# Linear attention's values loaded in one DMA over 128 partitions, and the order of turns drawn anew

## The chip, the cores and the metric

The kernel runs on one core of one Trainium2 chip. The metric is device time in microseconds; before the change the median of three runs is 1362.3 us (1359.67 to 1363.4). The core's engines are TensorE (PE), VectorE (DVE), ScalarE (ACT), GpSimd (POOL) and SyncE (SP, which here issues nearly all DMAs). Each takes its own instructions in order and waits on semaphores for the others.

## The reference

Eight batches of 256 tokens with 128 channels go through two layers; each layer adds two branches to its input. All is float32.

```
xn = layernorm(x)
x  = x + gla(xn) + local(xn)          # layer 0
xn = layernorm(x)
x  = x + delta(xn) + experts(xn)      # layer 1

gla (gated linear attention), per head (H = 4, Dk = 16, Dv = 32):
  S  = exp(gt)[..., None] * S + kt[..., None] * vt[..., None, :]
  ot = einsum('bhk,bhkv->bhv', qt, S)
  o  = rmsnorm(o) * g_norm_w * silu(x @ Wg);  return o @ Wo
local: two layers of windowed attention with a gated MLP
delta: delta rule in chunks of 32, two gates, state S passed from chunk to chunk
experts (8 heads, 8 experts, top 2 of 8 for values and for outputs):
  v   = einsum('bshep,bshe->bhsp', einsum('bsd,hedp->bshep', x, v_w), gate_v)
  att = softmax(q k / sqrt(P));  ctx = att v
  out = einsum('bshep,hepd->bsd', ctx[:, :, :, None, :] * gate_o[..., None], o_w)
```

## The kernel before, in words

**Gated linear attention.** The recurrence runs over time in the free dimension: for each pair of value channels j, j+1 one tile kv (128 partitions x 2 x 256) holds the values, repeated for each of the 16 key channels. Its 128 partitions are (half of the value channels, head, key channel): 2 x 4 x 16. ScalarE writes the values v of a batch to a tile, SP sends them to DRAM (`values`, L1775) and loads them back, repeated, into one of four kv tiles (`kvload`, L1791). VectorE multiplies by k (`gkv`, L1115) and scans over time with the decay (`gmul`, L1123, two scans), GpSimd multiplies by q (L1698), and TensorE sums over the key channels with a constant matrix `gla_sum` (L760, one group for two tiles). A batch has eight kv tiles; the loads of the fifth to eighth wait until the L760 group that reads the slot's earlier tile has run.

**Experts.** For each head and half of the experts (16 units for a batch, 128 in all) SP loads router weights repeated over all partitions, `vgate<-gates` (L1821) and `ogate<-gates` (L1833), and expert weights `wv`, `wo`. Three slots exist for each. GpSimd multiplies vgate by the input (L1748), TensorE makes the values (`hv`, L899, letter V), runs the attention (L910, L917, L927, L936, letter A), VectorE multiplies the context by ogate (L1352), and TensorE makes the output (`mproj`, L946, letter P). A V frees the value slot, a P the output slot, and only then SP issues the next load of that slot.

**Delta rule.** For each of the eight chunks TensorE's `du` (L827, state x winvT), VectorE's two products (L1294, L1296), TensorE's `ds` (L827, dlt x vkC), VectorE's sum into the state (L1305) and the next `du` follow each other; `dout` adds the output.

**The order.** No dependency sets the order of an engine's instructions: five strings do (TENSOR_TURNS, VECTOR_TURNS, SCALAR_TURNS, GPSIMD_TURNS, SYNC_TURNS). Each letter takes the next stage of one stream: a, b, c the local branch, G the linear attention, C the router, F and D the delta rule, A, V, P (W, O, v, o on the other engines) the experts, z the end of layer 0, E the store. BANK_TURNS gives each TensorE stage its PSUM bank. An engine that comes to a stage whose input is not there waits, with all that is queued behind it.

Of the kernel before, what the change touches and what calls it, by code (L numbers as in the profile page):

```python
# [37 lines left out]
def constants():  # L38

    i, j = np.arange(P)[:, None], np.arange(P)[None, :]  # L40
    out = {"ident": (i == j), "headsum": (i // DK == j // DK)}
# [46 lines left out]
    "VDaaDADDaaDaDDVDADDaAPPDbbDDaVDADDbaDaDDVDGaDDAVbbVDAbAbaPDAbbPFAbGbAAaAbVPPcaGVAcabAAVAPPcGbEaAbcAAGVGGacAaVG"
    "VAbbabbFFaPbAAbFAbPbVAbacGDaVcPaAAcVAPaVcAacPzPAAVAaCGaCVAPbAAaPbGPAPCVVVbbAabAAabAabVbFAGbaPbAAbGAbPDDcDaVDGc"
    "aDAVDDPDDAADcADDaVbbADPDDGbDVDDcDPDDAADaADDaaVDGAVFFDcGazPbbEbbFGPbbAAVbbAbDVPAVcCGVcGPVAAcPACVcAPPAAcAaPaCaAa"  # L90
    "AAPAPFPAaAAaAGPPADDaabVbVDaAADbVADDGGDVDAVVDDaDPDDAAaVbPbDDbDADbVDDbDDbaDbDDbabGDaAFaaPVAAaabbDAaPGGEbGFaPAFAA"
    "aVbbbAbPDbVbPbbcbGAcVPAAcVAcVAPccAAPcGAVcacAVcPzaAAPACGVCaPAVaaAAPVCGAaVbabPPDDAFADAabAVaDVGaDDGPDbbPDDbDbDDbb"
# [6 lines left out]
    "aaGbGbbcacbbcGbbaabccccaazGCCcaacGbcabbCCCbACCCCACGacccaGGcGzGCbCaGbbGGbGVCCCCCCCCVAOAVVOFcaaVVFcaacOFAOVVGGAF"
    "aaGbGabOaOGVVbAGbGGAFFFFDDbOOAbFVVADbcccbcGOOaaAVVAaaGFOAFAOFcOOVVcFcAVVAFFFFaaAFDAcccbDaDbbaVVDODbGDDDDODGDcb"  # L100
    "DGGbbDGDGDbGDGDaaGGDaOODADAcaVVGGcGcGaaDDGAaAaGVVGGDEbObbOcccabOOcAAzCCabOObACbCACbCCCCVVCaOOAaAFaaFDaVVGaGFDa"
    "DbcaDFbbOOVVbDDGDAcAcDDFDDFDOODGDGAGGAGDGGcccDGDGbVVDOObDcDzbVVCDbDCAFAFFEDOOcAaAaVVccVVOOAACCCCOOVVCCaCAaCAaa"
    "VVGGGGcccOcOAGDAGGGDDDaDaDDaaVVDODODbDbbDADbDAaDaVVDaDabDbDVVODbOAbAFFOOAaFAacFVVcbcabOOGAaAbEGbOOcVVccGcAAVVG"
    "bGGbbGGabaOFOAaAFGaGFGGFcFDGVVcGcDaOaOAGGADVVccccaazaCOOCAACCVVCCCOCCOCbAGGbbAGVVGbabOObAabAaVVbFFaOODAaFDAGcD"
    "FDcDcaVVDGaDODAOADbDbbDGDbVVDccDcDODOADaAaDDDVVFFczCCbEFbbFGbOGFGAGGAGGVVGGODDcaacDcGGVVOGGAOCCACCCcccCCVVOcAC"
    "AOGaaGOaAOAGaGFOOAaADaFFbDaaFVVbbDODObADADGVVDVVDDOObDDbDADbAVVDbDDaDaDaGDaFaDabOAabbAGEObaFFFOVVbOAbbFADDbDcc"
    "GVVcGGGOGAOAGGGVVcccGccOOccAAGaacccGVVGcGzCaCOaAOACCCCCVVCCCGGaAaOVVbOADbbGGbaDaFFDFVVDODAOFbDAGDbDbDDbDDDOODF"
    "DDGFDVVDGDFDAFADDFcDVVOOAcAcEVVOcccAOAczCCFVVOFACOACFCCCVVOCAOACFCVVDOOFDAFDAFFDFDVDVODODADADDDDVDVODODADADDDD"
# [12 lines left out]

GPSIMD_TURNS = (
    "aaaaaaababGGbabaGaGaGaaGaaGGbbbbGaaaaaaabaGbGGGabaabaGGaaGaaGbbbabaaGaaababaGWGWWbbGGWWWWaWWaaaGWaWabaGWabWGGb"
    "DWDDDDDWbDWWWaWaaDaDWaWaGWDbaDDbDaWDDDDDDbGDDGDDbGDaaGaWaWaDaGaGWWDbaGDbGDDbDWbDWaDaDaaWaWaDGaDbaWbWDDDDDDDDDD"
    "WGDGGDDGWbWbWDWDDDDWWWDWDDWDaWaaGDaDWDDaDaaDaGDWGDWDbDGDbDWDaDaaWDaWbWbaWaWabWaGbWWbWGabaGaaGGWDGWaWaDWaGaDDWW"
    "DDbGWbGDbDbDaWaaWaDWDDWDGaDWDDaDbWDbDDWDDDDaaWWbbGWGGGWDWDDDDDGDaDaGaGDaGaWWaWbaDaDWWWbDDWDWWDDDWbDDDDbDWDDaaa"
    "GaaaWbabaWbbDWDDWGGWGGWDDaWaDWaGaDWGDGaDWWWbbaaGDaDWDWDDbDDDbDDDWDDDGDWWDWWDWDWWDWWWDDDDDDWWDDWDDDDDWDDDDWDDDW"
    "DWDWDWDDWDWDDDWWWDDDDDDWDWDDDDDDDD")

SYNC_TURNS = (  # L130
    "xxxGGGGGGGGGGGGGGGGGGGGGGGCvvvooovvvGGvCvvGGoovvoovvovvoovvooovovvvvovoGGGGGoGGovvGGvvooEoxoooovoovCoovvvvooGG"
    "GGGvoovvvovoExoovvvoovvooGGvvGGCoovvoovvvvoovoovvooExvGGGvGGvoovGGvovovoovGGvooooCvvvvoovvovovovvGGGGoGEoxvvov"
    "GGvGGovovoooCooooovvvvvvovovovoEoGGvGGGovovovvooGGvvooGGvooCvvvoovvoovovvvvvovvEovvvoooooooCvvvoovoovvoovvovoE"
    "oovoovvoovvoooovvoooE")
# [10 lines left out]
    "26531746273514275425712347135131753175147157354514351403754130754107354107451347310473140143147137437140371437"
    "01475032471504750514765427507415743150714530745307451374105374105734073407354057034703543474357405764035764576"
    "37567304307634706343706370363760367103465710457031245013650136401340130173415347163471564731654016530615360143"
    "605463705167420536172506132706531705361750321573152071352703725")
# [1778 lines left out]
```

## Time and profile before

| | |
|---|---|
| median of 3 runs | 1362.3 us |
| the profiled execution | 1362.17 us |
| its span, first to last instruction | 1360.8 us |
| mean granted TensorE clock | 0.951 |
| PE, DVE, POOL, ACT busy | 89%, 71%, 62%, 53% |
| DMA engines: share of q1, bytes in all | 52.3%, 230.88 MB |

Shares are of the span. DMA share in a stretch is the mean over the core's 16 DMA engines. The granted clock is a share of 2.4 GHz: at 1.0 TensorE runs at 2.4 GHz, at 0.5 at 1.2 GHz. The chain of waits is followed back from the last instruction, at each step to what released it.

### The profile page before, as it was taken

Reading aid. Unit: us, or ns where it says so; the run is one execution under the profiler, and the core shown is the slowest. Engines: PE = TensorE matmul, PEld = TensorE weight load, DVE = VectorE, ACT = ScalarE, POOL = GpSimd, SP = SyncE. Lnnn points to the kernel's source line nnn. Section 1 sums busy time; section 2 is a strip of 40 time slices with the busy share of each in tenths; the row PEclk is TensorE's granted clock in tenths of the full one; section 3 lists DMA queues with packets and bytes.
Section 4 is the critical chain, followed back from the end, with each engine's and each line's share of the span. In section 5 each row is a group of like instructions: output and inputs, shape, how many; then the busy total and the mean of one; then the engine's idle time right before and its main releaser. Section 6 shows DMA issues by size and latency. Waiting matters only on the chain.

```text
span 1360.8 us, 31248 instructions
## 1 busy us (share of the span) xinstructions
PE 1207.0 (89%) x11890; PEld 955.2 (70%) x11890; DVE 962.8 (71%) x1950; ACT 722.1 (53%) x2060; POOL 847.7 (62%) x1157
## 2 busy tenths in 40 slices
...
GB/s 241 34 26 42 12 237 196 165 193 142 126 154 221 129 175 145 280 154 183 175 152 190 240 108 172 188 190 190 164 125 194 168 217 135 219 217 248 250 279 112
DMA packets 90675, 230.88 MB, mean 170 GB/s; under 512 B 9376, under 2 KB 15648, under 8 KB 90400
## 3 DMA queue, kind: packets, MB, share of 16 engines
q1 hardware_dynamic: 90384, 228.30, 52.3%
...
## 4 chain that ended last, share of the span: by engine, by line
PE 38%; DVE 25%; DMA 13%; ACT 12%; issue 7%; POOL 4%; SPq 1%; DVEq 0%; ACTq 0%; POOLq 0%
PE bank L899 9%; PE bank L946 8%; DMA ogate<-gates 7%; DVE ogate L1352 5%; DMA vgate<-gates 3%; PE bank L827 3%; DMA kv<-values 3%; DVE dy L1210 3%; PE bank L612 2%; ACT prob L1463 2%; PE bank L917 2%; PE bank L936 2%; POOL vgate L1748 1%; PE bank L927 1%; PE bank L707 1%
## 5 line engine op out<-in xcount | busy, mean ns | idle before, releaser
L1748 POOL TENSOR_TENSOR vgate<-vgate,xT 128x512 f32<-128x512 f32 x256 | 329.3, 1311 | 144.5 <-DMA vgate<-gates 144.2
L899 PE MATMUL bank<-wv,vgate 128*128 128x128 f32 x2048 | 264.4, 285 | 3.5 <-POOL vgate L1748 3.2
L899 PEld LDWEIGHTS bank<-wv,vgate 128*128 128x128 f32 x2048 | 254.6, 200 | 11.4 <-issue 6.8
L946 PE MATMUL bank<-ogate,wo 128*128 128x256 f32 x1024 | 251.6, 393 | 3.4 <-DVE ogate L1352 2.0
L946 PEld LDWEIGHTS bank<-ogate,wo 128*128 128x128 f32 x1024 | 195.2, 196 | 40.7 <-issue 14.3
L1352 DVE TENSOR_TENSOR ogate<-ogate,bank 128x1024 f32<-128x1024 f32 x128 | 153.3, 1213 | 49.6 <-DMA ogate<-gates 30.5
L1463 ACT ACTIVATE prob<-prob,mx 128x128 f32<-128x128 f32 (+1 forms) x256 | 96.0, 377 | 72.9 <-DVE mx L1059 72.7
L1630 ACT ACTIVATE mprob<-bank,mmin 128x256 f32<-128x256 f32 x128 | 59.4, 468 | 133.2 <-DVE mmin L1341 133.0
L1681 POOL TENSOR_TENSOR rot<-rot 128x512 f32<-128x512 f32 x64 | 81.7, 1277 | 65.5 <-DVE rot L1035 65.5
L612 PE MATMUL bank<-wqkv,hT 128*128 128x512 f32 x192 | 108.1, 664 | 4.5 <-ACT hT L1399 2.8
L1726 POOL TENSOR_TENSOR dlt<-dlt,step 128x126 f32<-128x126 f32 (+22 forms) x248 | 95.5, 385 | 19.4
L1698 POOL TENSOR_TENSOR kv<-kv,gq 128x512 f32<-128x512 f32 x64 | 82.3, 1291 | 33.8 <-DVE kv L1123 33.8
L1724 POOL TENSOR_TENSOR step<-dlt,uw 128x126 f32<-128x126 f32 (+22 forms) x248 | 90.9, 366 | 19.4 <-DVE dlt L1275 3.1
L1693 POOL TENSOR_TENSOR prob<-prob,rsum 128x256 f32<-128x256 f32 (+1 forms) x64 | 60.7, 951 | 57.7 <-DVE rsum L1062 57.5
L1688 POOL TENSOR_TENSOR rot<-rot,rn 128x512 f32<-128x512 f32 x64 | 68.8, 1075 | 28.1 <-ACT rn L1447 27.8
L1123 DVE TENSOR_TENSOR_SCAN kv<-bank,kv 128x256 f32<-128x256 f32 x128 | 81.0, 674 | 1.2
L936 PE MATMUL bank<-mprobT,vmoe 128*128 128x256 f32 x256 | 69.6, 395 | 6.0 <-ACT mprobT L1645 4.3
L917 PE MATMUL bank<-xT,mqk 128*128 128x256 f32 x256 | 69.0, 392 | 4.9 <-DVEq L1359 2.5
L1637 ACT ACTIVATE mprob<-mprob,msum 128x256 f32<-128x256 f32 x128 | 57.8, 500 | 26.3 <-DVE msum L1346 26.0
L1620 ACT ACTIVATE mqk<-bank 128x256 f32<-128x256 f32 x64 | 24.4, 381 | 74.5 <-PE bank L910 74.3
L1645 ACT ACTIVATE mprobT<-bank 128x512 f32<-128x512 f32 x64 | 37.9, 593 | 46.0 <-PE bank L927 45.5
L627 PE MATMUL bank<-small,rot 128*128 128x128 f32 x256 | 41.9, 288 | 20.4 <-POOL rot L1688 9.8
...
## 6 DMA issues: line engine op xcount, KB each, us to landing
vgate<-gates SPq DMA_DIRECT2D x128, 512.0 KB, 4.3
ogate<-gates SPq DMA_DIRECT2D x128, 512.0 KB, 4.4
wv<-in_wv_moe SPq DMA_DIRECT2D x128, 256.0 KB, 4.7
wo<-in_wo_moe SPq DMA_DIRECT2D x128, 256.0 KB, 4.9
kv<-values SPq DMA_DIRECT2D x128, 128.0 KB
...
x<-in_x SPq DMA_DIRECT2D x8, 128.0 KB, 3.2
```

Of the source, the lines that this page charges most:

```text
L612: nc.tensor.matmul(out, m.hT[:, n * P:(n + 1) * P], m.wqkv[:, l, k * INNER:(k + 1) * INNER], start=True, stop=True).then_inc(bank.filled, 1)
L899: i = nc.tensor.matmul(out[:, n * D:(n + 1) * D], xg[:, e, n * P:(n + 1) * P], m.wv[slot][:, e, :], start=(q, n, e) == (0, 0, 0), stop=(q, ...
L917: i = nc.tensor.matmul(out[:, n * T:(n + 1) * T], m.mqk[:, n * P:(n + 1) * P], m.xT[b % 2][:, :], start=True, stop=True)
L936: i = nc.tensor.matmul(out[:, 0:T], m.vmoe[:, k, h % 2, :], m.mprobT[:, k, :], start=k == 0, stop=k == 1)
L946: i = nc.tensor.matmul(out[:, 0:T], m.wo[slot][:, e, :], cg[:, e, :], start=(h, q, e) == (0, 0, 0), stop=(h, q, e) == (MH - 1, 1, EQ - 1))
L1352: i = tt(gate, gate, spread(out, 1, EQ), ALU.mult)
L1463: e = act(p[:, c, :], p[:, c, :], ACT.Exp, scale=-1.0, bias=top[:, c:c + 1], accum_out=rsum[:, c:c + 1])
L1681: tt(r, r, r2, ALU.add).then_inc(s.rot_added, 1)
L1698: tt(kv, kv, spread(m.gq[:, :], 1, 2), ALU.mult).then_inc(s.gmul, 1)
L1724: g.chain(tt(step, spread(m.solved[:, k // 2:, k], 2, k), spread(m.lanes[:, k, 0:k], 1, rows), ALU.mult))
L1726: i = tt(left, left, step, ALU.subtract)
L1748: i = tt(gate[:, e:e + half, :], gate[:, e:e + half, :], spread(m.xT[b % 2][:, :], 1, half), ALU.mult)
```

## The change

It has two parts. The first changes how the values come into the kv tiles. The partitions of kv are now (key channel, half, head), so that the repetition over key channels is the outermost dimension and one DMA fills all 128 partitions; the columns of the weights for q, k, the decay and v, and the matrix `gla_sum`, are put in the same order on the host. The second draws all five order strings and the bank string anew; each letter comes as often as before on every engine.

```diff
-    half, head = np.arange(P) // (GH * GK), np.arange(P) // GK % GH
+    half, head = np.arange(P) // GH % GVH, np.arange(P) % GH
...
 TENSOR_TURNS = (
-    "GaaaaGGGaaaaabbaXabbbbbaaaabbGbaabGbaaabbacaGGGbbcbbbbcbcbbcGbaaacGGGaacGaaabbccaabcGbbbaaabGbbaaaaabbGbabbcaG"
+    "GaaaaGGGaaaaabbXababbbbaGbababbabacaaacabGGbcacabGGcbbbaaabGbbaabbaaabbbGGaGcbGabcbbbcbcbGcbbGabaacaacGaaacbbc"
...
-        v.wait_ge(s.kv_in[slot], 32 * use)
+        v.wait_ge(s.kv_in[slot], 16 * use)
...
-        for a in range(GVH):
-            src = values_dram[b % 2].rearrange("(h a j) t -> a h j t", h=GH, a=GVH)[a, :, j:j + 2, :]
-            dst = m.kv[slot][a * GH * GK:(a + 1) * GH * GK, :, :]
-            nc.sync.dma_start(dst, spread(src, 1, GK)).then_inc(s.kv_in[slot], 16)
+        src = values_dram[b % 2].rearrange("(g j) t -> g j t", j=GJ)[:, j:j + 2, :]
+        nc.sync.dma_start(m.kv[slot][:, :, :], spread(src, 0, GK)).then_inc(s.kv_in[slot], 16)
...
-    twice = lambda w: np.tile(w, (1, GVH))
+    twice = lambda w: np.tile(w.reshape(-1, GH, GK).transpose(0, 2, 1)[:, :, None, :], (1, 1, GVH, 1)).reshape(-1, P)
...
-    a["gkb"] = np.tile(f["L0_attn_gk_b2"], GVH)[:, None]
-    a["gk1"], a["wv_gla"] = f["L0_attn_gk_w1"], f["L0_attn_Wv"]
+    a["gkb"] = twice(f["L0_attn_gk_b2"][None, :]).T
+    a["gk1"], a["wv_gla"] = f["L0_attn_gk_w1"], f["L0_attn_Wv"].reshape(D, GH, GVH, GJ).transpose(0, 2, 1, 3).reshape(D, P)
```

Two places of the order. The first is SP's queue where the first four kv tiles of the sixth batch are loaded (`x2` are the two halves of a tile; vgate and ogate with wv and wo are the loads of the experts). Before:

```order
L1821 DMA vgate0<-gates 128x1024
L1822 DMA wv0<-in_wv_moe 128x512
L1791 DMA kv0<-values 64x1x512 x2
L1791 DMA kv1<-values 64x1x512 x2
L1821 DMA vgate1<-gates 128x1024
L1822 DMA wv1<-in_wv_moe 128x512
L1791 DMA kv2<-values 64x1x512 x2
L1791 DMA kv3<-values 64x1x512 x2
L1833 DMA ogate0<-gates 128x1024
L1834 DMA wo0<-in_wo_moe 128x512
```

The same tiles in the changed kernel:

```order
L1819 DMA vgate1<-gates 128x1024
L1820 DMA wv1<-in_wv_moe 128x512
L1789 DMA kv0<-values 128x1x512
L1789 DMA kv1<-values 128x1x512
L1789 DMA kv2<-values 128x1x512
L1789 DMA kv3<-values 128x1x512
L1831 DMA ogate0<-gates 128x1024
L1832 DMA wo0<-in_wo_moe 128x512
L1831 DMA ogate1<-gates 128x1024
L1832 DMA wo1<-in_wo_moe 128x512
```

The four tiles now come together in four DMAs of 128 partitions, the vgate load that stood between them comes ahead, and two ogate loads follow.

The second is TensorE's queue where the first batch leaves layer 0 (`small,xn` is a transpose of normalized inputs, `gla,go` the linear attention's output, `xT,w_qk` and `xT,mqk` queries and scores of an expert head, `layer,xT` the router, L798). Before, up to the router:

```order
L779 MATMUL bank<-gla,go 128x128 x2
L910 MATMUL bank<-xT,w_qk 128x256
L647 MATMUL bank<-qkT 64x64 x8
L647 MATMUL bank<-qkT 64x128 x8
L752 MATMUL bank<-xn0T,gla 128x256
L917 MATMUL bank<-xT,mqk 128x256 x2
L732 MATMUL bank<-xn0T,gla 128x256
L733 MATMUL bank<-xn0T,gla 128x256
L798 MATMUL bank<-layer,xT 128x128 x2
```

In the changed kernel:

```order
L591 MATMUL bank<-small,xn 128x128 x2
L772 MATMUL bank<-gz,gla 128x256
L612 MATMUL bank<-wqkv,hT 128x512 x3
L591 MATMUL bank<-small,xn 128x128 x2
L779 MATMUL bank<-gla,go 128x128 x2
L752 MATMUL bank<-xn0T,gla 128x256
L910 MATMUL bank<-xT,w_qk 128x256
L671 MATMUL bank<-probT,vloc 64x64 x8
L798 MATMUL bank<-layer,xT 128x128 x2
```

The router matmul moves from row 136 to row 122 of TensorE's order: local attention of the second batch (L647, L627, L612, L691) that stood ahead of it now comes later.

## Rows read from the trace of the kernel before

**Rows 1.** busy time of the engines over the span, from the page
```profile
PE 1207.0 (89%) x11890; PEld 955.2 (70%) x11890; DVE 962.8 (71%) x1950; ACT 722.1 (53%) x2060; POOL 847.7 (62%) x1157
```

**Rows 2.** busy us of each engine by stretch, granted clock, DMA share, GB/s
```profile
0.00:200.00 200.00, 147.41 (x1152) 98.81 (x1153) 142.69 (x323) 146.11 (x440) 99.75 (x95) 0.88 0.27 97
200.00:1300.00 1100.00, 1004.46 (x10032) 811.14 (x10032) 792.95 (x1571) 560.46 (x1579) 722.30 (x1015) 0.96 0.58 182
```

**Rows 3.** the chain by line, shares of the span, from the page
```profile
PE bank L899 9%; PE bank L946 8%; DMA ogate<-gates 7%; DVE ogate L1352 5%; DMA vgate<-gates 3%; PE bank L827 3%; DMA kv<-values 3%; DVE dy L1210 3%; PE bank L612 2%; ACT prob L1463 2%; PE bank L917 2%; PE bank L936 2%; POOL vgate L1748 1%; PE bank L927 1%; PE bank L707 1%
```

**Rows 4.** long pieces of the chain that ended last: start, us, what
```profile
51.32 6.39 DMA kv<-values
...
222.84 10.63 DMA ogate<-gates
...
574.55 9.05 DMA kv<-values
...
887.11 15.13 DMA ogate<-gates
...
1090.46 9.39 DMA vgate<-gates
```

**Rows 5.** the same chain near 887 us, in full
```profile
881.25 0.53 SPq L1791
...
886.22 0.84 SPq L1791
...
902.27 1.23 DVE ogate L1352
```

**Rows 6.** PE in order of time, 897 to 907 us
```profile
897.72 1.89 PE L707 MATMUL bank<-hn,local 128*128 128x256 f32 x8
903.70 2.00 PE L707 MATMUL bank<-hn,local 128*85 128x256 f32 x4 [4.09 <-DVEq L1359]
```

**Rows 7.** DMA issues: KB each, median us from issue to landing
```profile
vgate<-gates SPq DMA_DIRECT2D x128, 512.0 KB, 4.3
...
kv<-values SPq DMA_DIRECT2D x128, 128.0 KB
```

**Rows 8.** landings of the ogate loads (L1833), min, median, max
```profile
DMA to landing us min/median/max: 3.5/4.4/15.1
```

**Rows 9.** two stretches of one us: kv loads alone, gate loads at full rate
```profile
29.00:30.00 1.00, 0.00 (x0) 0.00 (x0) 0.80 (x5) 1.00 (x4) 0.98 (x1) 1.00 0.27 98
...
221.00:222.00 1.00, 1.00 (x6) 0.89 (x5) 0.95 (x2) 0.00 (x0) 0.74 (x1) 1.00 1.09 432
```

**Rows 10.** eleven stretches around long waits for loads
```profile
222.00:239.00 17.00, 13.75 (x71) 10.22 (x70) 14.45 (x25) 9.56 (x22) 9.53 (x8) 0.91 0.73 238
...
887.00:908.00 21.00, 14.19 (x64) 11.14 (x64) 14.80 (x23) 6.16 (x15) 17.00 (x41) 0.77 0.73 213
...
sum 173.00, PE 137.08 PEld 109.67 DVE 124.34 ACT 81.39 POOL 95.56; mean PE 12.46 PEld 9.97 DVE 11.30 ACT 7.40 POOL 8.69
```

**Rows 11.** who waited for loads, us in total, times, longest
```profile
DVE kv L1115 <- DMA kv<-values: 22.9, 11, 4.9
```

**Rows 12.** PE's own waits: us in total, times, longest
```profile
PE bank L827 <- DVE dlt L1296: 7.5, 10, 2.8
...
PE bank L827 <- DVE state_sum L1287: 5.5, 4, 2.6
...
PE bank L827 <- POOL dlt_sum L1734: 4.9, 2, 4.5
PE bank L760 <- POOL kv L1698: 4.7, 3, 2.2
```

**Rows 13.** a stretch of the start, busy us
```profile
160.00:180.00 20.00, 13.71 (x88) 10.48 (x87) 17.13 (x48) 19.46 (x58) 6.69 (x7) 0.87 0.19 66
```

**Rows 14.** issue times of kv loads on SP (ns)
```profile
L1791 SPq DMA_DIRECT2D kv<-values x128: 509/511/1887, 21.1 to 1089.9; - x128
```

**Rows 15.** the output matmuls, busy and mean, idle before them
```profile
L946 PE MATMUL bank<-ogate,wo 128*128 128x256 f32 x1024 | 251.6, 393 | 3.4 <-DVE ogate L1352 2.0 <-DVEq L1358 1.3
```

More of the change, by code:

```diff
@@ L88 @@
[L88 to L92, printed above, removed]
@@ new lines @@
+    "DADGaDaaAbbaDDbacDGVbbVcaDDPAEAbcAPPbbVAbPbbVPAAGcAPPAVcaVzGaAAaAaGPVPAaaGVCVFAAaaAaCVaVPAPAAVAaVFFPADDbGGbDbG"
+    "bbbcDPbcDDAbVcbbDPcDDbbDcDDbzDADDbbDCGDDbADFDDPDAcDDAAVDAVcVPDDAVAAcVAPPEPCAVAACVAPPGcAVaAAaAaaPcPAVaaAACVAGaa"
+    "bPbaPAaVbAAaVbbbbaPbaPAabVbbaaabAcbbVcAGAFcAPcPDcDbVADGGDVDDADAVDDADPDDaDADPDDVDDaDGDDADAaVDDADaPbbbbAGVGGGbbD"
+    "AAFbbAFbPVEaFGVcGaADaVGcVaaPcPAAaVbbAGGaVbGPaVAaPAAcAGcVzAPaAbbbCPbCAabPbPbAbabFcCaacGAGAAVcAVcVPaPcADDAAzVDAa"
+    "DaPDbbDAPDaAbDDAaDADDFDaDFDDPDDADFDDAADGAVDDPaADVbbbbVDDbPbAbbAVbAcGCGPPEAcPAAVAcVCVcPVAcAAVAPPPACVAAVAPPAaVAA"
@@ L95 @@
+    "aAaaPAPAAGFAaaPPaAabbaVDDbaVGDAADGaDPbbbbAPbbDDGDDabbADabDDaDVDDaDaDDaDGbVbDADDAabDDPAaacDaFAVbbbbDcPDVbbEAbbA"
+    "cFbAcVAGFcGVcaVcaaPcGAVAVAcPPVcAaazAAVAPVaACabbCaPFAAPAaVVbAaPbbbbAAPbACVbVbPbAVbAAPAFFDDFVDGAVDVDDGcDVDDPDcVD"
+    "DPDADDAGDADDcVDPDDADGGDDAAVDAGPcDDAGVcPzVAACVACPPEPAVAAFACVPPAVAAVAPPFAFFAAAPPVDDAVDADADVDDADDPDPDDADVDDADADDV"
+    "DADDPDPDDAVDAAVPDDAPVVAAAAPPAEAAAPPAAAVAPPAAAAPPDADVDVAADVADDPDPADDVAADVADDPDPADDVAADVADDPDPADDVAADVADDPDPAADP"
     "PE")
 VECTOR_TURNS = (
-    "VaaaaaaaGaabaabbabGGabGGGbbaabGGaaGGGaaGGGaabGGGbbcbbcGbbcbccccGaacGaacaacbGaabbGGGbGcccGGcGbGaabGbaabGGGaaGGa"
@@ L99 @@
[L99 to L108, printed above, removed]
@@ L122 @@
-GPSIMD_TURNS = (
[L123 to L128, printed above, removed]
+    "VaaaaaaaGaabaabbaGGGbGbaGGbbGGbaaGGaaGGcacabcaabbGGGGbccccbGbaabGaabaabaabbGcGcGbbcGbGbGGbGGGccccGGaaGGcaaGcGG"
@@ new lines @@
+    "acaGbaaabbcccczaCGCGaabbGaaCCCaabCCCabaaCbACFFaAbFcbbGcFcaVVabGGaaGcccOOcGGzGCAGCAbGVVFbFaabaabOOAFGAFGbGFVVbb"
+    "GGbGcGOCcCCcCCObCVVCAbCAbDDGbDVVOOAAOOVVAAcccFcOFcVVFcaaAFcaaAOGVVcccaaOcAOAbaabbGODbOFFDAGDADDDGDFDbDaDaGDGDa"
+    "aGGDbbVVDGGODAOAbFaDaGFGDaaGGcDGDbDcVbbDDcbVGEGGADAObGGabOabVVbOOcccAAcVzVCCaaOAaaOAGaaVVGFFAaaOAOFVVCCCFVVCAO"
+    "ACOFDFCCDGCDbcbbDcbDOcbODVVbccDcbDcDbzDDDDGDACDAGCGDGGDcFGGDADOVDVcAGcFDDVVOOOGFAEAVVDOOACCaACaCCCcccCOOVVaaAC"
+    "AaacGGGGaaOOVVAbaaAGbbGGGbOOVVbbbaabaaAAaacbVcbbcVOObAFDcccAFFcDDFDGVDVODODADADDaDaDVDVDDGODODADADbDGbbVVbOGOF"
@@ new lines @@
+    "AGGGGGGGGaaVVAFGGGGcaaGDGcDcGGaaFEOOVbVFbbAabaaFAGGDOVOVcccAGcAzCCObVOVabbCCCbCCCCCAacAaFcacOOAaVVFAFcccDcFDOz"
+    "ODVAVCDaAaCbDbbDObDODaDADaDFAFDDDFDFDAOOADGFGDGDbDVbbVGDDbGGGGGOVVOAcDAGGGcGcGGGGAOAVVCCCCCcccCCVcVCOOAOAEVVOO"
+    "AaAaVVOOAaAaaaOOFAaAaFbDabbaFbDVVDODODFbGAbbADbDGaDaDDaaDDDaDabGVVDbbDOObDaaAAcDDDbcFbbDDcbVVEOOFAAcccFFcFVVcD"
+    "cacaOaVaVOGAGGAGGcccGGVVGGczaaOOACACVVbaabbCCCbCCACOACOCVbVFbbOAbOFAVFVFOODAFFADFFDVVFDGDGGGDcDGGDcGGDcDVDVODO"
+    "DAADDDDVVOODADGGDADDcccGDczCCOVOVACCCAECCCCCVVOAOAFFFVVOOAFAFFFVVOOAFDAFDDVDVODODADADDDDVDVODODADADDDDVVODODDA"
@@ new lines @@
+    "DAVVOOAAEVVOOAAOOAAOOADADVVDODOVVADADDODOVVADADDODOVVADADDODOVADADDDOOE")
+SCALAR_TURNS = (
+    "GaaaaaGGGaaaaGaaabaaababaXbbbabbabaabbbaaacaacaabcaaabcabGaGbabbGaabbbaaaababaabbGGaaaGacGbcbbbbcbbcbabbabaaca"
+    "aaacaaacbaacaaaGGaCGabCbaaCAaaaabaababGGGbaaAFbbCaaabbbAbacAFcaGFbcaacaAabFCAAbAabaaFbaabAbabbAAbFbbAbCcCaacba"
+    "AbcbbAAbbACbAbbAAbAAAAcAFAaacFcaaAGcaaAGFcAaaAaaAaAbaAaaGbAFDFDbAGAGGAaaGabaabbaabaAbbAaAaAFbaabbaaacDDbacbEAb"
+    "cAAbAbbabbAcAAAaCaAaaGAaaAGAaaGCFAaaaCAaAaaAFAFaAAFAFDDbGbbGbbcbbccbbbcbbbAbbCGbGACAAcADADcAAFAcEAACAACAaAcAaA"
+    "aaAaAAaaaaACaaaAbaAabAabAaabbbabbaabaAabbAabaAaacbcAbcFAcADDbFAGGFAAAaAaaGAaAaDADabbbAGbGGbbAFGbbAbEaaAFaAcaac"
+    "aacAaabGaFGbbAaAaGAaAcAAACaaCbbbCbbbAabbabFACcAaAaGGcAcAaacAaFADFDAaACaAabAbbaAFAaAaaFAAGAFAGaADDbbbbbbbbAbAcC"
+    "AEAcAcACAcAAAAACAAaAAaAaAAaAaAaaFaaAAaAaabDbDbaaaFAaaGGFbbbAbbbAGbabAbaaaaaaaabbbAaaAaAaaDAcDFbbbEcbbbbbAcbFAA"
+    "cAGGFacacacaGAaaGAcAAaaAACAaACaabCabAaFaAAbAabbbAbbCAbAbbAFbAFFADDAFAFccAcAAAGGADGDAAcACACCEAAAAFCAAAAFAFAFAFA"
+    "AFADDAAAAAAAAADDAAAAAAAEAAAAAAAAAAAADADAAAAAAAAAAAAAAADDAE")
@@ new lines @@
+GPSIMD_TURNS = (
+    "aaaaaaabaGbGGbGbaaGaaGaaabaGGbbaaGabaaaababGbGbGGGaaGaaGaaGabaGabaaaabaaabWWWbabaGaWaWWGGGbWaaabaGWGWbbGWbWDGb"
+    "DWWDDWWDWWDaDaaWaaWaDaDaGbbDDDDDDDaDaDGaDaGDbWWGDDbaDaGDaaGWbWDGGbDDWDWDGDWaWaaDaaWWaWaDaWWDbbGDbDbDDbDDDbDDDD"
+    "DDWDDWWGWGWGWWGWDDWWDDaWaaDaaWaWabaGbDDabaabaWDaGaWDWGGbbWDDWDDWDDWDDaDDaDDDGWDDWbbWGGGGaWaGGaWaGWaGWabWabaDGW"
+    "DDDDbWbDDaWaaDaWDWWDDWaDabDbDDaDDDaDDDDDDWGWbbWGGGDWDDDWGWWDWGWDGGWWDaDaaWaDaaabWabDWDDbDbDGaDDaDaDaDDWaDabDDW"
+    "baDaWbbWWDWDWaDWWaaDWaaWaDWababDWWbDbDWDGWGWGDGDWDWDWDGDWDGDGDWDDGDDDWDGWDDDWDWDWWDDDWDWWWDDDWDDWDDDDDDWDDDWDW"
+    "DWDDDDDDDDWWWDWDWDDWDDWDDWDDWDDDDD")
@@ L130 @@
 SYNC_TURNS = (
[L131 to L134, printed above, removed]
+    "xxxGGGGGGGGGGGGGGGGGGGGGGGCvvvooovvvoovGGGGovvoovvovCvoovvvvooovvooooGGGGGvvGGGGvvoEoxovovooovvovovvvvoooGGGGG"
@@ L137 @@
+    "ooCvvvovvvovvooEovxvooGGvoovCvGGoovvoovvoovvvoovvovGGGGGovGGvGGvvooEvxvovovooooCGvGGGGvvoovooovovvovGGGGooovvv"
+    "ovvoEooCxvvoovoooovvoovvovovEvGvGGGGvovvoovvovoovvooCvvovovGGvvGGvovovovovovvooEovCvoovvoooovvvoovvoovvoovvooE"
+    "oovoooovvvoovvoovoooE")
 BANK_TURNS = (
-    "76543210765204375643275062743503764257602356702367531072613051236750123675021435026742035425603742560372536053"
-    "76250735067502316705316072015637201560253064571320473215760140673740653174065317460517345174573670631756070156"
@@ L145 @@
[L145 to L148, printed above, removed]
+    "76543210765204375643275037265403726507365270632532072536017253617205365204136750124507351243601243560124356012"
```

33 lines of the change are left out of this document (12 added, 21 removed).

## The prediction

> **What bounds the kernel now.** I read the page's engine line first, then the stretches, then the chain of waits, then the pieces of that chain that are loads.
>
> TensorE is the bound: busy 1207.0 us of 1360.8 [rows 1], so 153.8 us idle. The stretches [rows 2] put 200 − 147.4 = 52.6 us of that in the first 200 us and 1100 − 1004.5 = 95.5 us between 200 and 1300. Its granted clock is 0.88 in the first stretch and 0.96 in the second, that is, part of the time at 1.2 instead of 2.4 GHz; (1 − 0.96) × 1100 = 44 us of the second at full-clock worth are lost too. No work is taken from TensorE by this change, so a gain can come only from these two: idle time and clock.
>
> The chain by line [rows 3] names the matmuls of the experts (9% and 8%) and, right behind, loads: ogate<-gates 7%, vgate<-gates 3%, kv<-values 3%. The pieces in order of time say which loads. Eleven pieces of the chain are waits of over 7 us for a load that was issued right behind a group of kv loads, or for kv loads themselves; first, longest and last are in [rows 4], the eleven sum to 107.9 us, the longest is 15.13 us. The reader is to see in [rows 5] what stands before the longest: eight kv issues of L1791 from 881.25 to 887.06, with one gate load between, then an ogate load that lands 15.13 us after its issue, and in [rows 6] TensorE idle for 4.09 us until VectorE's product with that ogate. The median for the same kind of load is 4.3 us [rows 7], its extremes 3.5 and 15.1 us [rows 8].
>
> Why: while kv loads run alone the DMA share is 0.27 at 98 GB/s, and while gate loads run it reaches 1.09 at 432 GB/s [rows 9]. 0.27 is close to four of sixteen engines (0.25), though two halves of a kv load, issued 0.5 us apart, are in flight together. So both halves take the same four engines, and a gate load that needs all sixteen ends behind them.
>
> By the Trainium skill, "DMA: Bandwidth & Descriptors", section "Why a DMA increments its semaphore by 16 and not by 1", a DMA takes the largest number of engines, at most 16, that divides both sides' slowest dimension, and always the lowest-numbered ones. The source of a kv load has 4 heads outermost, so 4 engines, the same for both halves: the trace agrees with its 0.27. The new source has the 16-fold repetition outermost and the destination 128 partitions, so 16.
>
> **What the change does, part by part.**
>
> 1. kv loads: 128 DMAs of 128 KB on four engines become 64 of 256 KB. The same bytes. Four old DMAs (two tiles, 512 KB, the usual group) take 512 KB / 98 GB/s = 5.3 us of four engines; spread as the gate loads are, whose destination also has 128 partitions outermost, they go at up to the 432 GB/s of [rows 9] and take 1.2 us of sixteen. A gate load behind such a group is up to 4.1 us earlier. SP issues 64 DMAs fewer at 0.51 us [rows 14], 33 us in all; SP mostly waits for free slots, so I cost this at nothing, except that each gate load behind a pair of tiles leaves 1 us earlier, which the 4.1 us contain roughly.
>
> 2. What that is worth on TensorE. In eleven stretches around those waits (wait, and a few us behind it; first, longest and sum in [rows 10]) TensorE is busy 137.1 of 173 us, 79.2%; in the rest of 200 to 1300 it is (1004.5 − 137.1) / (1100 − 173) = 93.6%. So the long waits cost 173 × 0.936 − 137.1 = 24.8 us of idle time, and about 5 us of clock (the clock of the eleven is short by 12.6 us in sum, where the average of the rest would give 5.9; both times 0.8 busy). 30 us against 107.9 − 11 × 4.35 = 60 us of landing over the median: half a microsecond of TensorE per microsecond of lateness. Nine of the eleven are gate loads: 9 × 4.1 × 0.5 = 18 us at best. Several lie where gate loads also queue behind each other (DMA share 0.73 in both stretches shown), which the change leaves, so I take two thirds, −12 us, and keep 0 and −25.
>
> 3. Waits for kv itself. VectorE waited 22.9 us in eleven times for kv loads [rows 11]; two are in the eleven pieces above (one is the 9.05 us of [rows 4]), and 51.32 in the start is a third. From 9.05 and 6.39 us to the 4.3 us of a gate load of twice the size. VectorE is not the bound; TensorE shows only 4.7 us of waiting for the products of kv [rows 12]. Bounds 0 and −12; I take −5, near the TensorE row.
>
> 4. The start. Before, the order gives TensorE about 119 us of matmuls (group means times counts) ahead of the first router matmul L798, now 108; the second batch's moves from 143 to 187. So expert work starts earlier, by at most 11 us of work, in a stretch where TensorE is 74% busy, which would bring 11 × 0.26 = 3 us. But ScalarE is busy 19.5 of 20 us there [rows 13], so it could also come to nothing, or cost a little if the chain rather than TensorE sets the start. −3, bounds +4 and −8.
>
> 5. Spacing of the experts. Three slots serve the gate loads, so an output product P (L946) can come only when the load issued behind the third P before has landed and been multiplied. Counted in matmul time from the order, 8 of 125 P had under 10 us for this, now 4; for the value matmuls 3, now 1. TensorE waited only 3.4 us before L946 [rows 15]: −2, bounds 0 and −4.
>
> 6. The delta chain. Between a chunk's L827 du and its ds, TensorE needs VectorE's two products; 20 of 56 pairs had under 2 us of other matmuls between, now 26. One such wait is 7.5 / 10 = 0.75 us [rows 12]. Six more: +4.5 us at most, +2 taken, 0 to +8 kept.
>
> Constants, weights and bias columns only change their contents: nothing. The wait count 16 for 32 is the same wait.
>
> Sum: −12 − 5 − 3 − 2 + 2 = −20 us. The profiled execution took 1362.17 us, 1.4 us around its span of 1360.8, and the median of the runs is 1362.3. 1362.2 − 20 = **1342 us**.
>
> **Rivals.**
>
> A. The loads were hidden, gain under 0.3%. For it: all loads of a kind wait behind slots, and SP spent its time waiting for products, not issuing; if a gate load lands 4 us earlier and TensorE still idles for VectorE or ScalarE (which between them make most of the entries in its wait list), only the bare TensorE waits go: 4.7 us for kv, and the drawn order returns +2 or more. About 1360 us. Against: the 4.09 us of [rows 6] sit directly behind a load. This is also what would come if the new loads did not use sixteen engines: then the plan, which counts on early kv tiles (in the sixth batch the third L760 group follows the first by 10 us of matmuls, before by 46), would wait, and it might be 1365.
>
> B. Slower: the delta chain is the new wait. Its place is L827, seven rounds for each batch, du, VectorE, ds, VectorE, du. The three largest waits at L827 are 7.5 + 5.5 + 4.9 = 17.9 us [rows 12]. If they grow by more than the count of tight pairs, say by half, and the POOL part too, that is +9 us, and ds behind a late du holds every expert matmul queued behind it on the in-order TensorE. It decides once the loads give less than 9 us: with a gain of 3 us from loads and nothing at the start, 1362 + 9 − 3 = 1368 us. Against: before, six of the eight tightest pairs lay in the last 300 us, where TensorE was as busy as elsewhere.
>
> C. More than forecast. If item 2 comes at its full 25 us, item 3 at 12 and the start at 8, less the +2: 1362 − 43 = 1319; half of the extra gives 1325. For it: after the long waits the chain holds more waits of 4 to 6 us for gates, which shrink a bit too, and less idle time keeps the clock at 2.4 GHz.
>
> **How the numbers follow.** Forecast (1328 to 1356): 0.58. A: 0.16. B: 0.14. C (below 1328): 0.12. The range 1326 to 1367 leaves out half of C and most of B, under 2 in 10. A measurement of this kernel tells 0.3% (4 us) from no change: below 1358.2 is faster, above 1366.4 slower. Faster 0.58 + 0.12 + 0.02 of A = 0.72; same 0.13; slower 0.14 of B and a little of A, 0.15.
>
> **What would show it.** Item 1: a stretch in which kv loads run alone shows a DMA share near 1, not 0.27, for a quarter of the time; the longest landing of ogate falls from 15.1 to some 10 us. Item 2: the chain holds less of ogate<-gates than 7% and fewer than eleven load waits over 7 us; TensorE's idle time between 200 and 1300 us falls from 95.5 to about 80. Item 3: VectorE's wait for kv falls from 22.9 to under 10 us. Items 5 and 6: waits before L946 no longer, before L827 up by a few us. I am wrong if landings fall and TensorE's idle time does not, or if it moves to L827 or to the first 200 us.

## The result, and the profile after

| | before | changed |
|---|---|---|
| median of 4 runs | 1361.0 us (1357.3 to 1363.4) | 1291.3 us (1287.8 to 1297.5) |
| ratio, 95% interval | | 0.9495 (0.9449 to 0.9541) |
| profiled execution, span | 1362.2, 1360.8 us | 1297.5, 1295.0 us |
| mean granted TensorE clock | 0.951 | 0.979 |
| TensorE idle | 153.8 us | 119.4 us |

The change takes 70 us, 5%, off; the forecast was 1342 us with a range down to 1326. The direction was right and the size was far off.

The busy line of the changed kernel, which answers to [rows 1]:

```profile
PE 1175.6 (91%) x11890; PEld 930.8 (72%) x11890; DVE 971.2 (75%) x1950; ACT 721.9 (56%) x2060; POOL 851.1 (66%) x1157
```

The span shrinks by 65.8 us, in two nearly equal parts: TensorE's idle time falls by 34.4 us, and the same 11890 matmuls take 31.4 us less busy time. The fall in busy time is the clock: busy time at a granted clock below 1, weighted by what is missing to 1 and summed over windows of 2 us, is 57.7 us before and 25.1 us now, 32.6 us less. The stretches, as in [rows 2] (busy us of the five engines, granted clock, DMA share, GB/s), show where it rose:

```profile
0.00:200.00 200.00, 152.74 (x1173) 101.78 (x1174) 153.08 (x336) 151.64 (x445) 108.17 (x100) 0.91 0.32 110
200.00:1235.00 1035.00, 967.50 (x10058) 783.34 (x10056) 789.94 (x1560) 556.14 (x1578) 724.53 (x1030) 0.99 0.59 191
```

The clock of the long stretch goes from 0.96 to 0.99, its idle time from 95.5 to 67.5 us. The window of one us in which only kv loads run, against the first row of [rows 9]:

```profile
26.00:27.00 1.00, 1.00 (x12) 0.98 (x10) 1.00 (x3) 0.96 (x6) 0.23 (x1) 1.00 1.02 287
```

The DMA share is 1.02 where it was 0.27, so all sixteen engines carry the load. The issues and the landings of the ogate loads, as in [rows 7] and [rows 8]:

```profile
vgate<-gates SPq DMA_DIRECT2D x128, 512.0 KB, 4.5
...
kv<-values SPq DMA_DIRECT2D x64, 256.0 KB, 4.5
```
```profile
DMA to landing us min/median/max: 3.6/4.2/10.2
```

The median landing of the gate loads hardly moves (4.4 to 4.2 us for ogate); the longest goes from 15.1 to 10.2 us. The waits of VectorE for loads, as in [rows 11] (us in total, times, longest):

```profile
DVE kv L1115 <- DMA kv<-values: 9.0, 5, 3.5
...
DVE ogate L1352 <- DMA ogate<-gates: 2.1, 3, 1.4
```

Before, the second of these was more than the 22.9 us for kv:

```profile
DVE ogate L1352 <- DMA ogate<-gates: 30.5, 13, 5.6
```

TensorE's own waits, as in [rows 12] and [rows 15]:

```profile
PE bank L946 <- DVE ogate L1352: 6.7, 6, 3.1
PE bank L827 <- DVE dlt L1296: 4.8, 9, 1.1
PE bank L827 <- DVE winvT L1279: 4.8, 3, 2.4
PE bank L760 <- POOL kv L1698: 3.2, 2, 3.0
```

L946 waits more than before (the group of [rows 15] had 3.4 us of idle time ahead of it, now 7.7), L827 less. The chain of this execution could be followed back for the last 890 us only (its shares add up to 68%); a second profiled execution of the same kernel, of 1288.2 us, has a whole one. Its shares by engine, and those by line, against [rows 3]:

```profile
PE 49%; DVE 34%; ACT 9%; issue 5%; DMA 2%; POOL 1%; DVEq 0%; ACTq 0%; POOLq 0%
PE bank L899 11%; PE bank L946 10%; DVE ogate L1352 5%; PE bank L827 4%; PE bank L612 4%; PE bank L936 3%; DVE kv L1123 3%; DVE dy L1210 3%; PE bank L917 2%; PE bank L927 2%; PE bank L671 2%; PE bank L647 2%; DVE kv L1115 1%; DVE prob L1055 1%; PE bank L707 1%
```

DMA is 2% of the chain where it was 13%, and no load is left in the list by line. Of the eleven pieces of over 7 us ([rows 4] has the longest) one has a successor; the longest loads of this chain are:

```profile
0.73 4.45 DMA gla<-in_gla
...
661.25 4.66 DMA kv<-values
...
1053.84 8.39 DMA kv<-values
```

### The profile page after: what moved, and what is told of

Read it like the earlier page. It is cut to its first block, busy times and chain, and to the rows that moved or that the text cites. A ratio compares the mean times of both kernels' runs of the same rounds, so it can differ in the third digit from the quotient of the medians.

```text
span 1295.0 us, 31167 instructions
## 1 busy us (share of the span) xinstructions
PE 1175.6 (91%) x11890; PEld 930.8 (72%) x11890; DVE 971.2 (75%) x1950; ACT 721.9 (56%) x2060; POOL 851.1 (66%) x1157
## 4 chain that ended last, share of the span: by engine, by line
PE 32%; DVE 24%; ACT 5%; DMA 4%; issue 3%; POOL 0%; DVEq 0%; ACTq 0%; POOLq 0%
PE bank L899 8%; PE bank L946 6%; DVE ogate L1352 5%; PE bank L827 3%; PE bank L936 2%; DVE dy L1210 2%; DVE kv L1123 2%; DMA kv<-values 2%; PE bank L612 2%; PE bank L917 1%; PE bank L927 1%; DVE mmin L1341 1%; PE bank L647 1%; DMA ogate<-gates 1%; PE bank L671 1%
## 5 line engine op out<-in xcount | busy, mean ns | idle before, releaser
L899 PE MATMUL bank<-wv,vgate 128*128 128x128 f32 x2048 | 257.5, 280 | 6.4 <-DVE prob L1055 2.4
L899 PEld LDWEIGHTS bank<-wv,vgate 128*128 128x128 f32 x2048 | 245.3, 194 | 17.4 <-issue 5.2
L946 PE MATMUL bank<-ogate,wo 128*128 128x256 f32 x1024 | 244.4, 385 | 7.7 <-DVE ogate L1352 6.7
L946 PEld LDWEIGHTS bank<-ogate,wo 128*128 128x128 f32 x1024 | 189.8, 191 | 40.6 <-issue 14.3
L612 PE MATMUL bank<-wqkv,hT 128*128 128x512 f32 x192 | 103.1, 635 | 3.6 <-ACT hT L1399 1.9
L1734 POOL TENSOR_TENSOR dlt_sum<-dlt 128x32 f32<-128x32 f32 x64 | 16.7, 260 | 75.5 <-DVE dlt L1296 75.5
L1033 DVE TENSOR_TENSOR rot<-bank,tables 128x512 f32<-128x512 f32 x64 | 43.7, 682 | 29.4 <-ACT ssq L1428 18.7
```

Of the source, the lines that this page charges most:

```text
L612: nc.tensor.matmul(out, m.hT[:, n * P:(n + 1) * P], m.wqkv[:, l, k * INNER:(k + 1) * INNER], start=True, stop=True).then_inc(bank.filled, 1)
L899: i = nc.tensor.matmul(out[:, n * D:(n + 1) * D], xg[:, e, n * P:(n + 1) * P], m.wv[slot][:, e, :], start=(q, n, e) == (0, 0, 0), stop=(q, ...
L946: i = nc.tensor.matmul(out[:, 0:T], m.wo[slot][:, e, :], cg[:, e, :], start=(h, q, e) == (0, 0, 0), stop=(h, q, e) == (MH - 1, 1, EQ - 1))
```

## The experiments

Each time is the median of the kernel's runs, each ratio is to the kernel before on the same chip, whose medians in these comparisons were 1355.8 to 1359.1 us.

**The loads alone.** `e1_load_only` has the new loads, weights and constants, with the order and the banks of before:

```diff
-        for a in range(GVH):
-            src = values_dram[b % 2].rearrange("(h a j) t -> a h j t", h=GH, a=GVH)[a, :, j:j + 2, :]
...
+        src = values_dram[b % 2].rearrange("(g j) t -> g j t", j=GJ)[:, j:j + 2, :]
+        nc.sync.dma_start(m.kv[slot][:, :, :], spread(src, 0, GK)).then_inc(s.kv_in[slot], 16)
```

> The new kv loads (one DMA over 128 partitions) with the order strings and banks of before. Theory L (most of the 70 us is the loads: gate loads no longer end behind kv loads on four engines, and my half a microsecond of TensorE for each microsecond of lateness was too small): 1300 to 1315 us, longest landing of ogate near 10 us, TensorE clock near 0.975. Theory O (my sizing of the loads was about right and the drawn order gives the rest): 1338 to 1345 us, longest landing near 10 us all the same, TensorE's idle time between 200 and 1300 us down by 10 to 15 us.

Measured: 1302.8 us, ratio 0.960 (0.955 to 0.964), as theory L has it. The loads alone are worth 56 us. Its busy line and stretches:

```profile
PE 1179.9 (90%) x11890; PEld 932.4 (71%) x11890; DVE 969.8 (74%) x1950; ACT 721.3 (55%) x2060; POOL 851.0 (65%) x1157
```
```profile
0.00:200.00 200.00, 147.98 (x1187) 98.79 (x1188) 145.75 (x326) 148.06 (x447) 102.22 (x96) 0.91 0.29 101
200.00:1304.00 1104.00, 1031.96 (x10704) 833.60 (x10702) 824.07 (x1625) 573.23 (x1614) 748.75 (x1062) 0.99 0.59 191
```

Idle time is 1304.0 − 1179.9 = 124.1 us, 29.7 less than before, and busy time is 27.1 less. In the first 200 us TensorE's busy time is the same (147.98 us against 147.41), with 1187 matmuls in it instead of 1152 at a clock of 0.91 instead of 0.88; the clock of the long stretch is 0.99. Its chain holds no load of over 7 us at all. With the order of before kept, one can follow where the lead grows, by the sending of the first batch's router gates to DRAM (`gates<-xn`) and the store of each batch: 1.6 us at the sending of the gates (174.8 against 176.4), 11.7 at the first store (394.1 against 405.8), 21.5, 24.2, 37.0, 48.9, 59.0, 56.4 and 56.7 at the others. It grows while kv loads of a later batch are issued among the gate loads, and not after the last of them, at 1090 us of before ([rows 14]).

**The order alone.** `e2_order_only` has the changed kernel's order and banks with the old loads of 64 partitions:

```diff
-        nc.sync.dma_start(m.kv[slot][:, :, :], spread(src, 0, GK)).then_inc(s.kv_in[slot], 16)
+        for a in range(GVH):
+            src = values_dram[b % 2].rearrange("(h a j) t -> a h j t", h=GH, a=GVH)[a, :, j:j + 2, :]
...
```

> The new order strings and banks with the kv loads of before (two DMAs on four engines). Theory L: 1340 us or more, since the order gives little by itself. Theory O: 1305 to 1318 us. A third, that the two need each other (an order drawn for tiles that land early loses with late ones): 1340 to 1375 us here while e1 also stays above 1335.

Measured: 1352.1 us over 10 runs, ratio 0.9966 (0.9935 to 0.9996). With the old loads the new order gains some 5 us, 1 to 9 by the interval. It brings its own waits for loads:

```profile
DVE kv L1115 <- DMA kv<-values: 39.6, 21, 5.5
```

39.6 us where before had 22.9: this order counts on early kv tiles. Against this kernel, the changed one gains 61 us by its loads.

**Eight engines.** `e3_eight` is the changed kernel with the 16-fold repetition behind (half, head), so that the source has 8 outermost. `e8_old_eight` is the same with the order of before. One DMA a tile, as in the change. Against sixteen engines only the number of engines differs (and the order of the partitions with it); against the old loads of four engines the number of DMAs is halved too:

```diff
-        nc.sync.dma_start(m.kv[slot][:, :, :], spread(src, 0, GK)).then_inc(s.kv_in[slot], 16)
+        nc.sync.dma_start(m.kv[slot][:, :, :], spread(src, 1, GK)).then_inc(s.kv_in[slot], 16)
```

> The new order, and each kv tile in one DMA whose source has 8 rows outermost, so that it should spread over 8 engines (DMA share near 0.5 while only kv loads run) with the partitions ordered as before. If the number of engines sets the price of a kv load: between e2 and the changed kernel, nearer to the changed one (half of the lateness of four engines is gone in full, a DMA fewer to issue). If it is the number of DMAs on SP's queue: equal to the changed kernel within 3 us. If kv loads matter little with the new order: all three alike.

> The order of before with kv loads on eight engines in one DMA for each tile. Four engines took 1359, sixteen 1303 us with this order; the new order took 1352, 1303 (eight) and 1291. If the cost goes with the time for which the engines are held (5.3, 2.6, 1.3 us for two tiles): (2.6 - 1.3) / (5.3 - 1.3) of 56 us are left, 1321 us. If only lateness over a slack of a few us costs: 1305 to 1312 us.

Measured: 1302.9 us (0.961, 0.956 to 0.967) and 1315.8 us (0.970, 0.963 to 0.977). While kv loads run alone in the second kernel, the DMA share is about a half:

```profile
24.00:25.00 1.00, 0.00 (x0) 0.00 (x0) 0.69 (x2) 1.00 (x6) 0.93 (x1) 1.00 0.46 133
```

So eight engines, with one DMA for each tile, bring some 43 of the 56 us in the old order, three quarters. In proportion to the time for which the engines are held it would be two thirds, 37 us and 1321 us, as expected; 1315.8 lies between this and the other expectation, and the interval (31 to 50 us) holds them both. So these runs don't tell whether the price is proportional. Four of the five runs of `e8_old_eight` lie at 1314 to 1318 us, and the profiled one, at 1302.7 us, is the fastest. By the Trainium skill, "DMA: Bandwidth & Descriptors", section "Why a DMA increments its semaphore by 16 and not by 1", the number of engines is the largest up to 16 that divides both slowest dimensions: 8 here, 4 before, 16 after. The trace agrees with 0.46, 0.27 and 1.02.

**Next to no kv bytes.** `e4_new_tiny` (changed order) and `e5_old_tiny` (order of before) load 8 KB instead of 256 KB a tile:

```diff
+            nc.vector.memset(tile[:, :, :], 0.0).then_inc(s.kv_zero, 1)
...
-        src = values_dram[b % 2].rearrange("(g j) t -> g j t", j=GJ)[:, j:j + 2, :]
-        nc.sync.dma_start(m.kv[slot][:, :, :], spread(src, 0, GK)).then_inc(s.kv_in[slot], 16)
+        src = values_dram[b % 2].rearrange("(g j) t -> g j t", j=GJ)[:, j, 0:16]
+        nc.sync.dma_start(m.kv[slot][:, 0, 0:16], spread(src, 0, GK)).then_inc(s.kv_in[slot], 16)
```

> The changed kernel with kv loads that bring only 16 time steps of one of the two channels (64 KB less than a thirtieth of the bytes; the linear attention's values are left out but for those). It bounds what kv loads still cost. Theory L: the loads that are left still cost, 1275 to 1285 us. Theory O: they cost nothing any more, 1286 to 1293 us.

> The order of before with kv loads of 64 KB less than a thirtieth of the bytes (16 time steps of one of two channels; the rest of the linear attention's values is left out). With four engines this order takes 1359 us, with sixteen 1303. If what counts is the time for which kv loads hold engines and late tiles, the last bytes give a little more: 1290 to 1298 us. If four engines had some other harm that is gone in full with sixteen: 1300 to 1303 us.

Both leave out the rest of the values, so their linear attention isn't that of the reference, and VectorE zeroes the four kv tiles once at the start. Measured: 1283.7 us (0.947, 0.942 to 0.952) and 1295.8 us (0.956, 0.950 to 0.964). By the medians the kv loads over sixteen engines still cost some 7 us in all in either order, though the intervals with and without them overlap, where those over four cost 63 (1359 against 1296) and 68 (1352 against 1284).

**What stands behind, or late kv tiles.** `e6_behind` tells these apart. It has the order of before and kv tiles by the new loads; behind each pair of tiles SP also issues the four old DMAs on four engines, to a spare tensor in DRAM that nobody reads. `e7_behind16` is its control, with the same bytes copied on sixteen engines:

```diff
+        for j in (j - 2, j) if j % 4 == 2 else ():
...
+            for a in range(GVH):
+                src = values_dram[b % 2].rearrange("(h a j) t -> a h j t", h=GH, a=GVH)[a, :, j:j + 2, :]
+                dst = spare_dram[n % 8][a * GH * GK:(a + 1) * GH * GK, :, :]
+                nc.sync.dma_start(dst, spread(src, 1, GK)).then_inc(s.spare_in[n % 8], 16)
```

The control against it:

```diff
-            for a in range(GVH):
...
+            src = values_dram[b % 2].rearrange("(g j) t -> g j t", j=GJ)[:, j:j + 2, :]
+            nc.sync.dma_start(spare_dram[n % 8][:, :, :], spread(src, 0, GK)).then_inc(s.spare_in[n % 8], 16)
```

> The order of before; the kv tiles come by the new loads on sixteen engines, and behind each pair of them SP issues the four old loads on four engines to a scratch tensor in DRAM that nobody reads. The kv tiles are there early; only what is issued behind is in the way. Theory G (the 56 us of the loads are gate loads that end behind kv loads on four engines): 1340 to 1365 us, longest landing of ogate above 13 us. Theory K (they are the kv tiles themselves being late for VectorE, which puts everything in its order late): 1303 to 1315 us, with the same long landings of the gates.

> The control of the run before: the same scratch copies of the same bytes, on sixteen engines. Theory G: 1305 to 1315 us, since 256 KB on sixteen engines hold each for about a microsecond. If it is as slow as the run before, it is bytes and writes to DRAM, not four engines, that cost there.

Measured: 1364.6 us over 10 runs, ratio 1.006 (1.003 to 1.009), and 1313.8 us, 0.965 (0.956 to 0.975): 51 us between the medians, 55 by the ratios. The control's four runs scatter, from 1304 to 1326 us. Both are as theory G has it; the longest landing of ogate is 13.7 us in the first and 9.8 in the control. The waits of VectorE and GpSimd for loads in the first (its lines are one number further on than before's):

```profile
DVE ogate L1353 <- DMA ogate<-gates: 41.5, 16, 8.9
DVE kv L1116 <- DMA kv<-values: 10.8, 7, 3.4
...
POOL vgate L1749 <- DMA vgate<-gates: 162.4, 52, 12.8
```

VectorE waits 10.8 us for kv tiles where it waited 22.9 before, and yet the whole of the old time is back: most of it goes to the gates. Not every kv tile is on time, for kv loads too are issued behind the copies of an earlier pair, and one of 11.81 us stands in the chain. That chain has nine pieces of over 7 us, eight loads and one store, some of them at the very places of before ([rows 4] has 222.84, 574.55 and 887.11):

```profile
223.77 8.91 DMA ogate<-gates
...
576.93 11.81 DMA kv<-values
...
867.12 10.13 DMA out<-x
...
896.46 11.64 DMA ogate<-gates
...
1040.75 12.95 DMA vgate<-gates
```

In the control the longest three are 7.22, 6.79 and 8.46 us, and the waits for ogate are 10.7 us:

```profile
DVE ogate L1353 <- DMA ogate<-gates: 10.7, 10, 2.5
```

What the comparison doesn't separate are SP's own issues: the first kernel has 64 more, of 0.62 us each, and SP's queue is 5% of its chain against 1%. The control bounds their price. It adds 64 issues, and their bytes, to the kernel with the loads alone:

```profile
L1796 SPq DMA_DIRECT2D spare<-values x64: 537/597/1317, 22.4 to 1034.4; - x64
```

By the ratios (0.965 against 0.960) that cost some 8 us. If the 64 more of e6_behind cost as much, which is an estimate, 47 of the 55 us are left for the four engines. And the number of issues isn't what made the kernel before slow: the control issues 128 DMAs of 0.60 us from `values`, the kernel before 128 of 0.51 us, and the control is 45 us faster.

**The pair again, for the order.** `a1_changed_again` and `a2_load_only_again` are the changed kernel and the loads alone, compared once more on one chip with 6 runs each; `e9_split` is the changed kernel with each vgate load in two halves that have a semaphore each, so that GpSimd can begin on the first:

```diff
-        nc.sync.dma_start(m.vgate[slot][:, :, :], rows(b, 0, h, q)).then_inc(s.v_in[slot], 16)
+        for sem, e in ((s.v_in, 0), (s.v_in2, EQ // 2)):
+            nc.sync.dma_start(m.vgate[slot][:, e:e + EQ // 2, :], rows(b, 0, h, q)[:, e:e + EQ // 2, :]).then_inc(sem[slot], 16)
```

> The changed kernel once more, to be compared with the next one in the same runs. The new loads alone gave a ratio of 0.960 to the kernel before and the whole change 0.950. If the drawn order is worth 11 us with the new loads: 1289 to 1293 us here, 1301 to 1305 us in the next. If the two were apart by chance: within 4 us of each other.

> The new loads with the order of before once more: 1301 to 1305 us if the order is worth 11 us, else within 4 us of the run above.

> The changed kernel with each vgate load in two DMAs of half the experts, each with its own semaphore, so that GpSimd can begin with the first half: GpSimd still waits 102 us for these loads. If that wait is on the path anywhere, a microsecond of each landing goes: 1280 to 1288 us. If GpSimd's wait is covered (TensorE waited for vgate products hardly at all), no change, 1288 to 1294 us; 128 more issues on SP could cost a little, up to 1296 us.

Measured: 1290.8 us (0.952, 0.949 to 0.955), 1301.5 us (0.960, 0.956 to 0.964) and 1291.9 us (0.954, 0.951 to 0.958). The order is worth 11 us once the loads are spread. Splitting gains nothing, though it works: GpSimd's wait for vgate, the largest wait for a load in the changed kernel, falls from 93.9 to 79.1 us.

```profile
POOL vgate L1751 <- DMA vgate<-gates: 79.1, 34, 8.2
```

That wait was covered: in neither the changed kernel nor its second execution does TensorE's list of waits ahead of L899 name GpSimd's product.

The experiments as a table, us, by the engines that a kv load takes and by order:

| order | 4 | 8 | 16 | 16, 8 KB a tile |
|---|---|---|---|---|
| of before | 1359 | 1316 | 1303 | 1296 |
| changed | 1352 | 1303 | 1291 | 1284 |

## Why the forecast was wrong, step by step

**Item 1, right.** Sixteen engines instead of four, share 1.02 for 0.27, longest ogate landing 10.2 us where "some 10" was said. e6_behind shows that most of the harm lay with what is issued behind. SP itself was held there too: of the 15.13 us at 887 us, the issue of the ogate load took 2.58, where its median is 0.32; in the changed kernel the longest such issue is 0.61.

```profile
887.11 2.58 SPq L1833 DMA_DIRECT2D ogate<-gates  x1
```

**Item 2, the step that failed.** It took −12 us, 25 at the very best, out of a price of half a microsecond of TensorE per microsecond of lateness. The loads alone gave 56 us, together with items 1 and 3. It failed at two places.

The first is how much of the eleven waits would go. Their stretches were reckoned short by 24.8 us of idle time, and the whole of e1_load_only has 29.7 us less idle time (38.3 in the profiled execution of a2_load_only_again, the same kernel): that reading was near, and rather low. But I multiplied it down, by 4.1 us of a mean excess of 5.5 a wait, and then by two thirds for gates that queue behind each other. In fact no load of over 7 us was left in e1_load_only's chain, where there had been eleven. My reason to scale down was that gates also queue behind each other; the longest ogate landing in e1_load_only is 11.1 us, so they do, but none of it stands in the chain with over 7 us.

The second is the clock: 5 us were reckoned, 27.1 measured as busy time. The sum over windows of 2 us, as above, is 57.7 us before and 28.9 us in e1_load_only, which confirms that this is clock. The 27 are at the upper end: the profiled execution of before had a mean clock of 0.951, the 37 executions of this kernel in the three comparisons had 0.954 to 0.967. Between the profiled executions of e6_behind and its control busy time differs by 18.4 us, idle time by 41.0. My stretches ended where TensorE's idle time ended. The rows of before across the wait of [rows 6] and beyond the end of the stretch 887:908 of [rows 10]:

```profile
898.00:900.00 2.00, 1.61 (x8) 1.08 (x6) 0.00 (x0) 0.86 (x4) 1.69 (x5) 1.00 1.02 260
900.00:902.00 2.00, 0.00 (x0) 0.00 (x0) 0.00 (x0) 0.00 (x0) 1.69 (x5) 0.91 0.87 298
902.00:904.00 2.00, 0.30 (x1) 0.30 (x2) 1.49 (x2) 0.00 (x0) 1.69 (x5) 0.50 0.28 112
904.00:906.00 2.00, 1.70 (x4) 0.58 (x3) 1.90 (x6) 0.60 (x2) 1.76 (x4) 0.50 0.26 103
906.00:908.00 2.00, 1.55 (x6) 1.50 (x7) 1.81 (x4) 1.97 (x4) 1.69 (x5) 0.50 0.19 73
908.00:910.00 2.00, 2.00 (x6) 1.56 (x6) 1.97 (x6) 1.98 (x4) 1.92 (x3) 0.50 0.01 2
910.00:912.00 2.00, 2.00 (x7) 1.62 (x6) 1.74 (x4) 0.71 (x2) 1.77 (x5) 0.53 0.12 16
912.00:914.00 2.00, 2.00 (x11) 1.77 (x10) 0.00 (x0) 0.00 (x0) 1.65 (x5) 1.00 0.85 238
```

TensorE is idle for about 4 us, and then runs for ten at 0.50, that is at 1.2 GHz. The last four of these, 908 to 912, lie outside my stretch and look like fully busy time: 2.00 of 2. The stall itself costs some 4 us; half clock on 0.30 + 1.70 + 1.55 + 2.00 + 2.00 = 7.6 us of matmuls costs almost 4 more, and no idle time shows it. The same place in e1_load_only, where the twelve matmuls of L707 now run on without the 4 us between them, and the idle time that is left is a later wait for ScalarE:

```profile
854.00:856.00 2.00, 1.90 (x9) 1.19 (x7) 1.69 (x4) 0.29 (x2) 1.69 (x5) 1.00 1.03 401
856.00:858.00 2.00, 0.64 (x5) 0.67 (x6) 1.81 (x6) 1.67 (x3) 1.76 (x4) 1.00 1.02 395
858.00:860.00 2.00, 2.00 (x11) 1.74 (x11) 1.93 (x5) 1.97 (x5) 1.69 (x5) 1.00 0.18 66
```

1.4 us idle, and the clock stays at 1.00. The forecast itself had written down that 44 us of the long stretch were lost to the clock, and then drew on 5 of them.

A better price stood in the same rows: the eleven pieces' excess over the median landing, 107.9 − 11 × 4.35 = 60 us, taken whole. A piece of the chain delays the end by its full length if nothing else comes up close behind it. For profiled executions with a whole chain and the order of before, by 4.35 us for each piece:

| kernel | excess of chain loads over 7 us | its time |
|---|---|---|
| before | 60 us | 1362 us |
| e6_behind | 52 (57 with its store) | 1366 |
| e8_old_eight | 16 | 1303 |
| e7_behind16 | 7 | 1306 |
| a2_load_only_again | 4 | 1299 |
| e1_load_only | 0 | 1305 |

It parts the kernels near 1364 us from those near 1303. Within 0 to 16 us it orders nothing (the median of e8_old_eight is 1316 us, 13 above this execution), and that 60 comes so near to 56 may be in part luck: part of the excess was covered (24.8 us were idle), and the clock came on top.

**Item 3, in the direction.** VectorE's wait fell from 22.9 to 9.0 us as said, TensorE's for L760 from 4.7 to 3.2. In e1_load_only VectorE's wait is 4.2 us and TensorE's 4.6. Its share of the 56 us isn't measured apart; that e6_behind has most kv tiles early and still the old time suggests that it is small.

**Item 4, −3 taken, −8 the bound.** The order gave 11 us with the loads spread. The changed kernel has 152.7 us of busy time on TensorE at 200 us, e1_load_only 148.0, and sends the first router gates at 163.8 us where e1_load_only does at 174.8. Of the 9.0 us between the two profiled spans, 4.7 are idle time, all of them in the first 200 us, and 4.3 busy time. That the start gives all 11 isn't shown: no kernel has the new start with the old rest, and that stays open.

**Items 5 and 6, both the wrong way.** Waits ahead of L946 were to shrink and rose from 3.4 to 7.7 us; L827 was to cost 2 us more; its wait for dlt fell from 7.5 to 4.8 and that for state_sum from 5.5 to 0.7, while that for winvT rose from 1.2 to 4.8. Counting matmul time between two letters of the order doesn't tell which of them will wait when every landing time changes.

**The rivals.** A, that the loads were hidden, falls with e1_load_only. B, the delta chain, never showed. C, more than forecast, had the right sign and 12 in 100, and even its full −43 us was too little, since it had the same 5 us of clock in it. Its sum has a slip as well: 43 is 23 us more than the 20 forecast, and half of that gives 1331 us, not 1325.
